# Perceiver stack on one core: the second layer's first two blocks in one stage each, projections moved from the middle chain beside its maxima, a row bias, and unread products left out

## The chip, the cores and the metric

One core of one Trainium2 chip. The metric is the device time of one execution in microseconds (us), median of the runs. Engines: PE is TensorE, DVE is VectorE, ACT is ScalarE, POOL is GpSimd, SP is SyncE, which issues the DMAs.

## The reference

Two layers over a state `x` of 128 rows and 256 columns. Each layer is cross attention of `x` on a context of 12544 rows, then a small self block, then a feed forward block with quantised weights. Cut to what matters:

```
x = x + L0_xattn(ln(x), ctx, mask)       # 16 heads of 16, keys 12544, mask, softmax
x = x + L0_attn(ln(x))                   # causal linear attention, its FFN (gelu)
x = x + L0_ffn(ln(x))                    # bit-linear: gate, up, down
x = x + L1_xattn(ln(x), ctx, ctx)        # 16 heads, keys 12544, no mask
x = x + L1_attn(ln(x))                   # RWKV mix: Wk, Wv, Wr, a scan over the rows, Wo
x = x + L1_ffn(ln(x))                    # bit-linear w1, conv over 3 rows, silu, w2
```

In cross attention `q = (ln(x) Wq + bq) * 0.25`, keys `ctx Wk + bk`, values `ctx Wv`, and the softmax over all 12544 keys is made block by block with a running maximum for each head and query.

## The kernel before, in words

The keys are cut into 98 tiles of 128, these into blocks of 8 tiles, NG = 13 blocks a layer (the last of 2 tiles). Block m of layer l is m = NG * l + n, so blocks 0 to 12 are layer 0, block NG = 13 is the first of layer 1. All engines run programs written out by hand with semaphores. For each tile PE makes

- `scores`: first the running maximum is subtracted by a product with `minus16` (L1574), then keys times queries (L1578) into the four banks of `ps_scores`; ACT takes the exponential (L821; in layer 0 with a mask added before it);
- `weigh` (L1599) of the tile before: values times probabilities, added up in `ps_out`;
- `projections`: one unit, either 512 columns of keys of block m + 2 (`keys_in`, L1516) or two tiles of values of block m + 1 (`values_in`, L1501), in four strips of 32 into `ps_proj`;
- `maxima`: products of rounded keys and queries (L1523), whose largest over 512 keys VectorE finds (L1099 in layer 0, L1102 in layer 1). A block has 32 of them, for the block after: the table `count_at(m, t)` says how many stand behind the scores, behind the weighing and at the end of tile t, for this block (`own`), the next (`now`) and the one after (`ahead`).

When a block's 32 maxima are done VectorE joins them to the running maximum (`chain`, L1143), ACT rounds it (`max_out`, L773), PE spreads it over rows (`turn_max`, L1618), ACT copies it (`rows_out`, L797), POOL takes the change and ACT its exponential (`decay_out`, L789), and VectorE scales `ps_out` by it (`decay_sums`, L1166). This is a stage. In layer 0 and for most of layer 1 a stage is a block. Blocks NG and NG + 1 are **split** in two stages of four tiles (`is_split`, SPLIT = 4, `CHAINS`): before layer 1's first tile only the 16 maxima over block NG's first four tiles are made, two at a time (`pair_maximum`, L1134), and its other 16 go behind its tiles 0 to 2 (`own`).

Between the layers lies the **middle chain**: a chain of small steps of PE, VectorE and ACT (self block and feed forward). PE fills its waits in program order with projection units of blocks NG, NG + 1 and NG + 2, here at full width (`keys_whole` L1487, `values_whole` L1477): `BETWEEN` lists 13 of them, `between_in(...)` places them, ACT copies them out (`between_out`). Three more, in strips, stand beside the pair maxima (`BESIDE`, after pairs 2, 5 and 7).

Behind the last tile comes the **closing chain**: the last weighing, the turn of the sums (L1610), `wo` (L1463), the RWKV products (L1855, L1860, L1862), the products by `w1` (L1876), the convolution's PE half (L1885), the turns of the hidden rows (L1890, L1896) and `w2` (L1901). `idle_products(n)` (L1677) issues n products of 256 columns whose result nobody reads; one of them shows as two MATMUL instructions in the trace, as every f32 product does.

At the start SP loads, in this order: x, Wq, Wk, bk, half of the first context block, bq (one row of 256 copied to all 128 partitions, L481), the other half, the mask, Wv and so on. VectorE adds bq to the query product (L1216) and scales the two halves into `qz` (L1223). PE's order there is: query product, the first key unit, the turn of `qz` (L1703), the second key unit, then the maxima.

`lends(m, t)` picks maxima of layer 1 that ACT copies out of PSUM first (L764), so that VectorE reads the copy (L1109).

## Time and profile before

| | us |
|---|---|
| median of 3 runs (963.69 to 967.66) | 963.81 |
| the profiled execution | 969.17 |
| its span, first to last instruction | 966.3 |
| PE busy | 924.5 (96%) |
| VectorE busy | 755.6 (78%) |
| ACT busy | 697.8 (72%) |
| POOL busy | 398.6 (41%) |

The span divides into: the start up to the first tile (38 us), layer 0's tiles (to 461 us), the middle chain (462 to 510), the pair maxima (510 to 520), layer 1's tiles (521 to 925) and the closing chain (925 to 966). The chain of waits that ended last is 83% PE, 7% VectorE, 3% ACT. An engine's busy share says what it did, not what it held up; the chain says the latter.

### The profile page before, as it was taken

The numbers are of one execution on the slowest core, as the hardware profiler recorded it, in microseconds if no ns is written. First come the engines' busy times: TensorE is split into PE (matmuls) and PEld (weight loads), VectorE is DVE, ScalarE is ACT, GpSimd is POOL, SyncE is SP. The second block draws the span as 40 slices with busy tenths as digits, with TensorE's granted clock in tenths as the row PEclk, the third lists the DMA queues.
The fourth block names the chain that finished last, engine by engine and source line by source line (L and its number), as shares of the span: only waits on it lengthen the run. The fifth ranks groups of instructions, "written<-read, shape, count | busy, mean of one in ns | idle before, by whom it ended". The sixth has DMA issues, their size and how long they took to land.

```text
span 966.3 us, 37466 instructions
## 1 busy us (share of the span) xinstructions
PE 924.5 (96%) x16290; PEld 572.3 (59%) x16291; DVE 755.6 (78%) x1610; ACT 697.8 (72%) x1005; POOL 398.6 (41%) x365
## 2 busy tenths in 40 slices
PE   7999999999999999999888899999999999999987
PEld 3455665665656566655563556666666666666666
DVE  5888888888888888967446988777777778777666
ACT  3678998998998899897563456666666666666752
POOL 4368888788888877886100010021202000110000
PEclk9999999999999999999997999999999999999999
DMA  8411201201211110123005001011101101000000
GB/s 337 165 42 67 88 26 68 90 24 68 89 60 55 67 58 8 68 91 134 6 26 193 2 2 46 3 45 46 45 4 46 46 3 46 14 3 3 3 1 6
DMA packets 14995, 53.08 MB, mean 55 GB/s; under 512 B 4336, under 2 KB 5744, under 8 KB 10992
## 3 DMA queue, kind: packets, MB, share of 16 engines
q1 hardware_dynamic: 14832, 50.70, 15.1%
q8 instruction: 128, 2.10, 0.9%
q14 instruction: 35, 0.29, 0.1%
HBM read 50.56 MB, written 0.13 MB: 52 GB/s over the span
## 4 chain that ended last, share of the span: by engine, by line
PE 83%; DVE 7%; issue 5%; ACT 3%; DMA 1%; POOL 0%; SPq 0%; DVEq 0%; POOLq 0%; ACTq 0%
PE ps_out L1599 18%; PE ps_scores L1578 16%; PE ps_proj L1501 15%; PE ps_proj L1516 14%; PE ps_max L1523 7%; PE ps_scores L1574 4%; DVE tile_max L1102 2%; ACT probs L821 1%; PE ps_proj L1523 1%; DVE probs L1194 1%; PE ps_scores L1516 1%; DMA bq<-in_L_xattn_bq 1%; DVE unread L1099 1%; PE ps_out L1477 1%; PE ps_max L1477 1%
## 5 line engine op out<-in xcount | busy, mean ns | idle before, releaser
L637 POOL TENSOR_TENSOR probs<-probs,masks 128x512 f32<-128x512 f32 x180 | 227.3, 1284 | 76.3 <-ACT probs L807 76.3
L815 ACT ACTIVATE probs<-probs 128x1024 f32<-128x1024 f32 x196 | 206.7, 1055 | 44.7 <-DVE probs L1183 34.1
L1578 PE MATMUL ps_scores<-q_pad,k_full 32*128 32x256 f32 x3072 | 237.3, 378 | 0.0
L1099 DVE CUSTOM_DVE_ANT_0 unread<-ps_max,masks 128x512 bf16<-128x512 f32 (+1 forms) x294 | 190.5, 675 | 49.1 <-PE ps_max L1523 48.2
L821 ACT ACTIVATE probs<-ps_scores 128x1024 f32<-128x1024 f32 x192 | 186.3, 1021 | 44.8 <-PE ps_scores L1578 44.4
L1599 PE MATMUL ps_out<-probs,values 128*32 128x128 f32 x6272 | 217.1, 277 | 1.6 <-DVE ps_out L1166 0.5
L1578 PEld LDWEIGHTS ps_scores<-q_pad,k_full 32*128 32x128 f32 x3072 | 187.0, 187 | 12.5
L1599 PEld LDWEIGHTS ps_out<-probs,values 128*32 128x32 f32 x6272 | 159.3, 110 | 57.3 <-issue 50.4
L1501 PE MATMUL ps_proj<-wv,ctx_t 128*32 128x256 f32 x2752 | 165.3, 381 | 0.2
L1523 PE MATMUL ps_max<-k_high,q_high 32*128 32x512 bf16 (+1 forms) x579 | 153.2, 382 | 8.5 <-DVE tile_max L1099 3.2
L1516 PE MATMUL ps_proj<-ctx_t,wk 128*32 128x512 f32 (+1 forms) x1360 | 159.8, 587 | 1.0 <-DVE tile_max L1099 0.8
L628 POOL CAST k_high<-k_full 128x1024 bf16<-128x1024 f32 (+1 forms) x51 | 50.2, 988 | 215.6 <-DVE k_full L1118 116.5
L1102 DVE TENSOR_REDUCE tile_max<-ps_max 128x1 f32<-128x512 f32 (+1 forms) x202 | 134.0, 671 | 6.0 <-PE ps_max L1523 5.2
L643 POOL TENSOR_TENSOR max_step<-max_rows 128x512 f32<-128x512 bf16 x26 | 30.1, 1159 | 214.2 <-ACT max_rows L797 214.2
L1574 PE MATMUL ps_scores<-max_rows,minus 32*128 32x512 bf16 x768 | 109.9, 382 | 6.5 <-ACT probs L821 4.4
L1523 PEld LDWEIGHTS ps_max<-k_high,q_high 32*128 32x128 bf16 x579 | 37.7, 91 | 132.0 <-DVE tile_max L1099 52.9
L1501 PEld LDWEIGHTS ps_proj<-wv,ctx_t 128*32 128x32 f32 x2752 | 81.8, 110 | 50.1 <-DVE tile_max L1099 0.8
L1183 DVE TENSOR_TENSOR probs<-ps_scores,masks 128x1024 f32<-128x1024 f32 x90 | 109.7, 1219 | 0.0
L764 ACT CAST unread<-ps_max 128x512 bf16<-128x512 f32 (+1 forms) x79 | 45.6, 577 | 83.9 <-PE ps_max L1523 83.9
L807 ACT COPY probs<-ps_scores 128x512 f32<-128x512 f32 x180 | 95.4, 584 | 1.4 <-PE ps_scores L1578 1.3
L1102 DVE TENSOR_REDUCE tile_max<-ps_proj 128x1 f32<-128x512 f32 (+1 forms) x103 | 69.4, 674 | 15.0 <-PE ps_max L1523 8.0
L1523 PE MATMUL ps_proj<-k_high,q_high 32*128 32x512 bf16 (+1 forms) x193 | 72.3, 375 | 3.2 <-DVE tile_max L1102 3.2
(308 smaller groups left out, 940.8 us busy)
## 6 DMA issues: line engine op xcount, KB each, us to landing
ctx_t<-in_ctx_t SPq DMA_DIRECT2D x23, 1024.0 KB, 5.9
masks<-in_mask_n SPq DMA_DIRECT2D x12, 512.0 KB, 3.7
masks<-in_mask_t SPq DMA_DIRECT2D x12, 512.0 KB, 3.9
room_w<-in_L_attn_f_w SPq DMA_DIRECT2D x2, 1024.0 KB, 7.0
room_w<-in_L_ffn_w SPq DMA_DIRECT2D x2, 1024.0 KB, 8.1
ctx_t<-in_ctx_t SPq DMA_DIRECT2D x2, 512.0 KB, 5.7
room_w<-in_L_ffn_w_gate SPq DMA_DIRECT2D x1, 1024.0 KB, 11.1
room_w<-in_L_ffn_w_up SPq DMA_DIRECT2D x1, 1024.0 KB, 13.6
```

The source lines that it names most:

```text
L637: nc.gpsimd.tensor_tensor(p, p, three(mask_t[m % 2], GT)[:, t, :].unsqueeze(1).to_broadcast([P, 4, P]), ALU.add).then_inc(sig("bias_added" ...
L815: nc.scalar.activation(prob(T, half), prob(T, half), ACT.Exp).then_inc(sig(f"exp_done{half}"), 1)
L821: nc.scalar.activation(prob(T, half), scores_in(m, t, half).rearrange("p a n -> p (a n)"), ACT.Exp).then_inc(sig(f"exp_done{half}"), 1)
L1099: ins = v.tensor_tensor_reduce(unread[:, j % 2, 0:width(m)], max_bank(m, j)[:, 0:width(m)], mask_n[m % 2][:, half_cols(m, half)], 1.0, -3e ...
L1102: ins = v.tensor_reduce(tile_max[:, h, 1 + half:2 + half], max_bank(m, j)[:, 0:width(m)], AX_X, ALU.max)
L1183: v.tensor_tensor(prob(T, 0).rearrange("p (h q) -> p h q", h=8), ps_scores[:, 0:2, :].rearrange("p a (h q) -> p (a h) q", q=P), three(mask ...
L1501: last = mm(bank[32 * g:32 * (g + 1), D * (t - at.start):D * (t - at.start + 1)], ctx_t[m % 3][:, t, c, keys], wv[l][:, c, :], start=(c == ...
L1516: last = mm(bank[32 * g:32 * (g + 1), 0:width(m)], wk[l][:, c, dims], ctx_t[m % 3][:, 4 * half:min(4 * half + 4, size(m)), c, :], start=(c ...
L1523: mm(bank[:, 0:width(m)], q_high[rows, c, zz, :], k_high[m % 2][rows, c, half_cols(m, half)], start=True, stop=True).then_inc(sig("max_rea ...
L1574: mm(banks[g], minus16[rows, :], max_rows[stage(m, t) % 2][rows, :], start=True, stop=True)
L1578: last = mm(banks[g][:, D * c:D * (c + 1)], k_full[m % 3][rows, c, P * t:P * (t + 1)], q_pad[rows, c, :], start=False, stop=True, skip_gro ...
L1599: last = mm(ps_out[VW * g:VW * (g + 1), P * c:P * (c + 1)], values[m % 2][:, t, h, :], prob(T, half)[:, P * o:P * (o + 1)], start=(t == 0 ...
```

## The change

Six parts:

1. **One stage for each of the blocks NG and NG + 1.** `is_split` is always false, `CHAINS` is empty. All 16 pairs of maxima of block NG are made before layer 1's first tile; its 32 maxima for block NG + 1 go 4, 6, 6, 6, 4, 4, 2 behind tiles 0 to 6, and block NG + 1 has the table of the later blocks. Two chains, turns, row copies and scalings go.
2. **Projections.** `BETWEEN` has 9 units in place of 13, `BESIDE` 7 in place of 3, one after each odd pair from 1 to 13.
3. **Idle products.** All 44 calls behind layer 1's last weighing and in the closing chain are left out. Before `turn_max` of the opening there are 7 in place of 1, and 2 new ones behind it.
4. **bq of layer 0** is loaded as one row of one partition, second behind Wq, and added by PE with a product of one row of ones. VectorE's addition goes.
5. `lends` asks that the next tile has a projection (three copies by ACT for the last two blocks' maxima go, and block NG + 1 has six where it had four), and layer 0's late addition of `bv` and scaling of layer 1's bq (L1263, L1265) move from block NG - 2, tile 4, to block NG - 3, tile 3.
6. PE's wait for `sums_taken` behind the sums of layer 0 goes; in ACT's program some copies of units stand behind the step of the chain that they stood ahead of; pairs of waits ahead of one instruction change places.

```diff
-        bq = [sb(f"bq{l}", [P, D]) for l in range(2)]
+        bq_row = sb("bq_row", [1, D])
+        bq = sb("bq", [P, D])
...
         def is_split(m):
-            return m in (NG, NG + 1)
+            return False
...
-        CHAINS = {(NG, SPLIT - 2): NG + 1, (NG, 5): NG + 2, (NG, 7): NG + 3}
+        CHAINS = {}
...
             if m == NG:
-                own = ((2, 2, 2), (2, 2, 2), (2, 2, 0))[t] if t < SPLIT - 1 else own
-                now = ((0, 0, 0), (0, 0, 0), (0, 0, 4), (2, 2, 2), (2, 2, 2), (2, 2, 2), (2, 2, 2), (2, 2, 0))[t]
-            elif m == NG + 1:
-                now = (2, 2, 2) if t in (2, 4) else (2, 0, 2) if t < chain_at(m) else (2, 0, 0) if t == chain_at(m) else now
+                now = (2, 2, 2) if t in (1, 2, 3) else (2, 0, 2) if t < chain_at(m) else (2, 0, 0) if t == chain_at(m) else now
...
-            if m <= NG or k >= BLOCKS or lone(k, s):
+            if m <= NG or k >= BLOCKS or lone(k, s) or not (keys_at(k, s) or values_at(k, s)):
...
-        BIAS_AT = NG - 2
+        BIAS_AT = (NG - 3, 3)
...
-        BETWEEN = [("k", NG + 1, 0), ("k", NG + 1, 1), ("v", NG, 0), ("v", NG, 1), ("v", NG, 2), ("k", NG + 1, 2), ("k", NG + 1, 3),
-                   ("k", NG + 2, 0), ("v", NG, 3), ("v", NG + 1, 0), ("v", NG + 1, 1), ("v", NG + 1, 2), ("k", NG + 2, 1)]
+        BETWEEN = [("k", NG + 1, 0), ("k", NG + 1, 1), ("v", NG, 0), ("k", NG + 1, 2), ("k", NG + 1, 3), ("v", NG, 1),
+                   ("v", NG, 2), ("v", NG, 3), ("k", NG + 2, 0)]
-        BESIDE = [("k", NG + 2, 2), ("k", NG + 2, 3), ("v", NG + 1, 3)]
-        BESIDE_AT = (2, 5, 7)
+        BESIDE = [("k", NG + 2, 1), ("v", NG + 1, 0), ("k", NG + 2, 2), ("v", NG + 1, 1), ("k", NG + 2, 3), ("v", NG + 1, 2), ("v", NG + 1, 3)]
+        BESIDE_AT = (1, 3, 5, 7, 9, 11, 13)
...
+                if l == 0:
+                    project(ps_proj[:, 0:D], wq[0], whole=False)
+                    pe.wait_ge(sig("q_bias0"), 16)
+                    pe.wait_ge(sig("ones_set"), 1)
+                    mm(ps_proj[:, 0:D], ones[0:1, :], bq_row[0:1, :], start=False, stop=True).then_inc(sig("q_ready"), 1)
...
                 if l == 1:
-                    idle_products(1, ps_proj)
+                    idle_products(7, ps_proj)
                 turn_max(NG * l, ps_proj)
...
+                    idle_products(2)
...
-                    between_in(0, 1, 2)
-                pe.wait_ge(sig("sums_taken"), l + 1)
+                    between_in(0, 1)
...
-                    between_in(4)
...
-                    between_in(5, 6)
+                    between_in(3)
...
-                    between_in(9, 10, 11)
+                    between_in(6, 7)
...
-            idle_products(1)
+            pe.wait_ge(sig("sums_taken"), 2)
...
-            idle_products(3)
...
-            idle_products(4)
...
-            idle_products(18)
...
-            idle_products(7)
...
-            idle_products(2)
...
-                idle_products((1, 6)[half])
```

How the instructions stand, at three places. On SP at the start, before:

```order
L521 DMA x<-in_x 128x256
L510 DMA wq<-in_L_xattn_Wq 128x512
L515 DMA wk<-in_L_xattn_Wk 128x512
L516 DMA bk<-in_L_xattn_bk 128x2
L495 DMA ctx_t<-in_ctx_t 128x1024
L481 DMA bq<-in_L_xattn_bq 128x256
L495 DMA ctx_t<-in_ctx_t 128x1024
L500 DMA masks<-in_mask_n 128x1024
```

and now:

```order
L516 DMA x<-in_x 128x256
L505 DMA wq<-in_L_xattn_Wq 128x512
L518 DMA bq_row<-in_L_xattn_bq 1x256
L510 DMA wk<-in_L_xattn_Wk 128x512
L511 DMA bk<-in_L_xattn_bk 128x2
L490 DMA ctx_t<-in_ctx_t 128x1024 x2
L495 DMA masks<-in_mask_n 128x1024
```

The broadcast of 128 rows ahead of the second half of the context is gone; Wk, bk and the first half each stand one issue later, the second half where it stood.

On PE in layer 1's opening, from the pair maxima (k_high, q_high) to the first tile's scores (rows of wk and wv are units of `BESIDE`, those of wq and ident are idle products), before:

```order
L1523 MATMUL ps_scores<-k_high,q_high 128x512 x4
L1523 MATMUL ps_max<-k_high,q_high 128x512 x2
L1516 MATMUL ps_out<-ctx_t,wk 32x512 x8
L1523 MATMUL ps_scores<-k_high,q_high 128x512 x4
L1523 MATMUL ps_max<-k_high,q_high 128x512 x2
L1516 MATMUL ps_proj<-ctx_t,wk 32x512 x8
L1523 MATMUL ps_scores<-k_high,q_high 128x512 x4
L1501 MATMUL ps_out<-wv,ctx_t 32x256 x16
L1677 MATMUL ps_proj<-wq,ident 128x256
L1618 MATMUL ps_proj<-ident,max_of_head 32x128 x16
L1574 MATMUL ps_scores<-max_rows,minus 128x512 x4
```

and the last part of it now:

```order
L1515 MATMUL ps_scores<-k_high,q_high 128x512 x4
L1493 MATMUL ps_out<-wv,ctx_t 32x256 x16
L1515 MATMUL ps_max<-k_high,q_high 128x512 x2
L1515 MATMUL ps_scores<-k_high,q_high 128x512 x2
L1669 MATMUL ps_proj<-wq,ident 128x256 x7
L1610 MATMUL ps_proj<-ident,max_of_head 32x128 x16
L1669 MATMUL ps_out<-wq,ident 128x256 x2
L1566 MATMUL ps_scores<-max_rows,minus 128x512 x4
```

Ahead of this part stand 24 maxima and six units, so that 32 maxima and seven units now precede the first scores, where 16 and three did.

On PE in the closing chain, from `wo` to the products by w1, before:

```order
L1463 MATMUL ps_proj<-wo,xn_t 128x256 x2
L1677 MATMUL ps_out<-wq,ident 128x256 x3
L1452 MATMUL ps_max<-ident,xn 128x128 x2
L1677 MATMUL ps_out<-wq,ident 128x256 x4
L1855 MATMUL ps_scores<-room_t,room_w 128x128 x12
L1677 MATMUL ps_out<-wq,ident 128x256 x18
L1860 MATMUL ps_proj<-room_w,room_t 128x256
L1862 MATMUL ps_proj<-room_w,room_t 128x256
L1677 MATMUL ps_out<-wq,ident 128x256 x7
L1866 MATMUL ps_max<-ident,room_t 128x128 x2
```

and now:

```order
L1455 MATMUL ps_proj<-wo,xn_t 128x256 x2
L1444 MATMUL ps_max<-ident,xn 128x128 x2
L1849 MATMUL ps_scores<-room_t,room_w 128x128 x12
L1853 MATMUL ps_proj<-room_w,room_t 128x256
L1855 MATMUL ps_proj<-room_w,room_t 128x256
L1858 MATMUL ps_max<-ident16,room_t 128x128 x2
```

Only the products that are read are left.

## Rows read from the trace of the kernel before

**Rows 1.** Start, DMA issues at 3.09 and 3.56 us (size, us to landing)
```profile
bq<-in_L_xattn_bq SPq DMA_DIRECT2D x1, 128.0 KB, 6.7
...
ctx_t<-in_ctx_t SPq DMA_DIRECT2D x1, 512.0 KB, 7.6
```

**Rows 2.** Start, timeline (start us, us, engine, line, operation, [idle before])
```profile
6.94 1.92 PE L1516 MATMUL ps_scores<-ctx_t,wk 128*32 128x512 f32 x16
...
9.90 0.42 DVE L1216 TENSOR_TENSOR room_t<-ps_proj,bq 128x256 f32<-128x256 f32 x1 [4.66 <-DMA bq<-in_L_xattn_bq]
...
10.78 0.66 PE L1703 MATMUL ps_max<-ident,room_t 128*128 128x128 f32 x4 [1.91 <-DVE room_t L1223]
```

**Rows 3.** Middle chain, timeline of PE and VectorE (DVE)
```profile
465.93 0.41 DVE L1302 TENSOR_SCALAR xn<-x,stat 128x256 f32<-128x256 f32 x1
...
466.15 1.89 PE L1477 MATMUL ps_max<-wv,ctx_t 128*128 128x256 f32 x8
...
474.59 0.42 DVE L1320 COPY room_t<-ps_proj 128x256 f32<-128x256 f32 x1 [0.86 <-PE ps_proj L1789]
...
479.57 1.88 PE L1487 MATMUL ps_max<-ctx_t,wk 128*128 128x512 f32 x4
...
479.87 0.41 DVE L1031 TENSOR_SCALAR xn<-room_t,stat 128x256 f32<-128x256 f32 x1
...
500.62 0.43 DVE L1067 TENSOR_SCALAR masks<-probs 128x512 bf16<-128x512 f32 x1
```

**Rows 4.** Second layer's opening, timeline: pair maxima, a projection, an idle product
```profile
510.53 2.36 DVE L1134 TENSOR_REDUCE tile_max<-ps_scores 128x2 f32<-128x1024 f32 x2 [1.92 <-PE ps_scores L1523]
...
516.66 1.93 PE L1501 MATMUL ps_out<-wv,ctx_t 128*32 128x256 f32 x32
...
518.52 0.70 PE L1677 MATMUL ps_proj<-wq,ident 128*128 128x256 f32 x2
...
521.34 0.62 PE L1574 MATMUL ps_scores<-max_rows,minus 32*128 32x512 bf16 x4 [0.74 <-issue]
...
525.48 1.22 PE L1677 MATMUL ps_out<-wq,ident 128*128 128x256 f32 x2
```

**Rows 5.** Three stretches: us, busy us of PE, PEld, DVE, ACT, POOL, granted clock, DMA
```profile
517.95:521.36 3.41, 1.69 (x34) 0.71 (x27) 1.91 (x3) 1.49 (x4) 0.00 (x0) 1.00 0.53 144
521.36:531.60 10.24, 9.39 (x85) 5.37 (x85) 5.06 (x8) 5.26 (x6) 0.00 (x0) 0.50 0.14 57
925.00:966.30 41.30, 33.61 (x199) 26.56 (x195) 27.29 (x83) 14.72 (x27) 3.08 (x5) 0.99 0.01 4
```

**Rows 6.** PE timeline: first rows of tiles, and the turns of the maxima (L1618)
```profile
547.65 0.50 PE L1574 MATMUL ps_scores<-max_rows,minus 32*128 32x512 bf16 x4
...
551.35 0.50 PE L1574 MATMUL ps_scores<-max_rows,minus 32*128 32x512 bf16 x4
...
557.57 0.41 PE L1618 MATMUL ps_max<-ident,max_of_head 128*32 128x128 bf16 x16
...
593.76 0.41 PE L1618 MATMUL ps_max<-ident,max_of_head 128*32 128x128 bf16 x16
...
627.28 0.41 PE L1618 MATMUL ps_max<-ident,max_of_head 128*32 128x128 bf16 x16
...
880.05 0.60 PE L1574 MATMUL ps_scores<-max_rows,minus 32*128 32x512 bf16 x4
...
883.35 0.40 PE L1574 MATMUL ps_scores<-max_rows,minus 32*128 32x512 bf16 x4 [0.50 <-ACT probs L821]
```

**Rows 7.** PE timeline of the closing chain
```profile
934.79 2.94 PE L1855 MATMUL ps_scores<-room_t,room_w 128*128 128x128 f32 x24 [0.55 <-DVE room_t L1372]
...
937.57 7.94 PE L1677 MATMUL ps_out<-wq,ident 128*128 128x256 f32 x36
...
951.33 1.07 PE L1876 MATMUL ps_scores<-xn_t,ctx_t 128*128 128x128 bf16 x16
...
956.58 0.66 PE L1890 MATMUL ps_scores<-ident,masks 128*128 128x128 f32 x4 [0.23 <-ACT masks L993]
```

More of the change, by code:

```diff
@@ L196, in is_split @@
         def is_split(m):
-            return m in (NG, NG + 1)
+            return False
         def stage(m, t=0):
-            return m + max(0, min(m - NG, 2)) + int(is_split(m) and t >= SPLIT)
+            return m
         def in_stage(m, t):
@@ L206, in block_of @@
         def block_of(s):
-            m = s - max(0, min((s - NG + 1) // 2, 2))
-            return m, is_split(m) and stage(m) == s
+            return s, False
         def tiles_to(s):
@@ L296, in count_at @@
                 now = (2, 0, 2 if t < chain_at(m) else 0)
-            if m == NG:
-                ahead = (0, 0, 2) if t == size(m) - 1 else ahead
-            elif n + 2 < NG:
+            if n + 2 < NG:
                 ahead = (0, 0, 2) if t == chain_at(m) else (2, 0, 2) if t > chain_at(m) else ahead
@@ L342, in perceiver @@
         for l in range(2):
-            done = {NG * l: (2 * H, H)[l]}
-            read = {bank: ("max_free", maxima0(NG * l) + (2 * H, H)[l]) for bank in range(2)}
+            done = {NG * l: 2 * H}
+            read = {bank: ("max_free", maxima0(NG * l) + 2 * H) for bank in range(2)}
             order, turned_here, moved = [0, 1, 2], {}, 0
@@ L511, in load_q_weights @@
                 if l == 1:
-                    row(bq[l][:, :], f"L{l}_xattn_bq", D, "q_bias1")
+                    row(bq[:, :], f"L{l}_xattn_bq", D, "q_bias1")
             def load_k_weights(l):
@@ L522, in _ @@
             load_q_weights(0)
+            sp.dma_start(bq_row[:, :], a["L0_xattn_bq"].rearrange("(o n) -> o n", o=1)).then_inc(sig("q_bias0"), 16)
             load_k_weights(0)
             load_first_ctx(0)
-            row(bq[0][:, :], "L0_xattn_bq", D, "q_bias0")
             load_first_ctx(1)
@@ L1233, in _ @@
                 else:
-                    for i in range(H // 2):
+                    for i in range(H):
                         pair_maximum(NG, i)
@@ L1459, in turn_apart, with project @@
                 return last
-            def project(dst, w, src=xn_t):
+            def project(dst, w, src=xn_t, whole=True):
                 for c in range(DC):
-                    last = mm(dst, src[:, c, :], w[:, c, :], start=(c == 0), stop=(c == DC - 1))
+                    last = mm(dst, src[:, c, :], w[:, c, :], start=(c == 0), stop=whole and c == DC - 1)
                 return last
@@ L1698, in _ @@
                 if l == 1:
[L1699 to L1700 removed]
+                    between_read(7)
+                    between_read(8)
                 for zz in range(2):
@@ L1720, in _ @@
                 else:
-                    for i in range(H // 2):
+                    for i in range(H):
                         pair_maximum(NG, i)
@@ L1724, in _ @@
                             beside_in(BESIDE_AT.index(i))
-                    beside_read(1)
+                    for u in (len(BESIDE) - 2, len(BESIDE) - 1):
+                        if u % 2 == 1:
+                            beside_read(u)
                 read_by[0] = ("max_copied", NG * l + 1)
                 if l == 1:
-                    idle_products(1, ps_proj)
+                    idle_products(7, ps_proj)
                 turn_max(NG * l, ps_proj)
                 if l == 1:
-                    beside_read(2)
+                    for u in (len(BESIDE) - 2, len(BESIDE) - 1):
+                        if u % 2 == 0:
+                            beside_read(u)
+                    idle_products(2)
                 if l == 0:
```

66 lines of the change are left out of this document (29 added, 37 removed).

## The prediction

> **What bounds the kernel now.** I read the page first: PE is busy in 96% of the span and makes 83% of the chain of waits, so in the long run of tiles only PE's own work counts, and there the change does nothing. What it touches are four places where PE is not the whole chain: the start, the middle chain, layer 1's opening and the closing chain. For each I read the timeline of PE beside those of VectorE and ACT, and for the clock the table of stretches.
>
> At the start VectorE has the query product at about 7.4 us and waits until 9.9 for bq, whose copy to 128 partitions lands 6.7 us after its issue; the second half of the context is queued behind it and lands at 3.56 + 7.6 = 11.2 us [rows 1, 2]. In the middle chain the small steps are often ready before PE has ended the full-width unit ahead of them: ln1's result is there at 466.34, a unit begun at 466.15 ends 1.7 us later; ln2's is there at 480.28, a unit begun at 479.57 is ahead of it [rows 3]. In the opening VectorE's reductions follow each other without a hole (about 1.14 us a pair, two in 2.36), and PE has time for units beside them [rows 4]. Then the clock: in 517.95 to 521.36 PE was busy for half the time, at full clock, and the next 10.2 us were granted 0.50, the lower of the two levels (1.2 GHz of 2.4), though PE was busy for 9.4 of them. The closing chain is at 0.99 [rows 5].
>
> **The change part by part.** All times against the profiled execution (969.17, span 966.3), which lies 5.4 us above the median of the runs; I take the same difference for both.
>
> *Start: -1.4.* The query product ends where the first unit begins now, at 6.94, and the row bias adds one product, two instructions of 0.215 [rows 7] (36 in 7.94, with the end of the last): q is ready at 7.4. VectorE's 0.42 addition and its wait to 9.9 go, and PE's turn of qz then stands behind its own first unit, 7.4 + 1.9 = 9.3, where it began at 10.78 [rows 2]: 1.45 earlier. The second unit needs the context's second half by 10.0 and not by 11.4. I take it that it lands in time, since the 128 rows of bq that held the queue are gone; Wk and the first half come one issue later (0.47) and are not late. Bounds: 0.2 if that half lands where it did, 1.45. In the Trainium skill, "DMA: Bandwidth & Descriptors", section Specifications, pieces of 512 bytes or more move at line rate; by that bq's 1 KB rows took some 0.3 us of the queue, the half would land at 10.9 and this part would give 0.5, not 1.4. The rows speak for more: bq, a quarter of the half's size, landed 6.7 us after its issue, and the half only 1.4 us behind it.
>
> *Middle chain: -4.7.* Four units of 1.72 leave it (6.9 us of PE). In each gap I let PE begin the next step at the later of its units' end and its input [rows 3]. First gap, three units to two: the turn waited for the third unit to 467.9, its input is there at 466.34, but ACT first copies the second unit (0.7 from 466.3): 1.3. Behind the attention product (a unit fewer): the copy that PE must wait for ends at 475.01, and PE, in a unit since the product ended (about 474.5), came to it at 476.2: 1.15. Before ln2's turn: 481.3 against 480.28: 1.1. ACT's new order ahead of the quantised rows: 0.2. Before the turn of the hidden rows (three units to two): the second half's input is there at 501.05 and PE was some 0.9 behind it. Sum 4.7; bounds 3.9 (ACT's copies in the way each time) and 6.9.
>
> *Opening: -0.8.* The pairs: 16 x 1.14 = 18.3 us in place of 9.15, all VectorE. Beside them PE makes seven units of 1.86, 13.0 us, and has 5.3 for 32 small products, as before 3.6 for 16 [rows 4]: VectorE stays the bound, +9.15. The seven idle products are 3.0 us and begin about 2.4 before VectorE ends, so they end with the rounding of the maxima; the two behind the turn take 0.86 where ACT's row copy took 0.7: +0.2. Then the first block's tiles. Before, from 521.34 to the turn of the next block's maxima at 557.57, they took 36.2 [rows 4, 6] at 48 maxima, 10 us of it at the lower level. Now: 32 maxima. A tile with six is 3.7 (547.65 to 551.35, VectorE's bound), one with four and no projection 3.3 (880.05 to 883.35, where PE waited for ACT) [rows 6]. 3.3 + 3 x 3.7 + 3 x 3.3 for tiles 0 to 6 and 1.7 of tile 7 up to the turn = 26.0: -10.2. I take the full clock: PE is dense through the pairs. Bounds of this part: +4 (the lower clock for the same 10 us) and -3.
>
> *Block NG + 1: -2.7.* From turn to turn it took 593.76 - 557.57 = 36.2, the next block 627.28 - 593.76 = 33.5 [rows 6]. The table is now the same, and the scaling within the block is gone. Bounds 0 and 2.7.
>
> *Small parts: +0.3.* VectorE's 1.3 us for `bv` and bq moves from a tile where it had an idle stretch behind it to one where it has 0.6: 0 to 0.7. The copies that `lends` drops stood while ACT waited for PE: nothing. Two turns, copies and scalings fewer are in the two blocks above. Waits that change places: nothing.
>
> *Closing chain: +5.8.* The 44 idle products are 88 x 0.215 = 18.9 of the 33.6 us that PE is busy there [rows 5, 7], and one call, between the two turns of the hidden rows (0.43), is on the path. Without them PE is busy for 14.7 of 41, 36%, less than the half that went before the fall in the opening. So I expect the lower level from about 929 on. What streams then doubles, of it on the path: the turn ahead of wo and wo itself 0.11 + 0.86, the next turn 0.21, the first 8 of the 24 RWKV products 8 x 0.107 = 0.86 (the other 16 stay hidden behind VectorE's scans), two products of Wo 0.86, the small turns 0.15, 8 of the 16 by w1 0.43: 3.5. The 24 products of the convolution ended just before ACT released the turns at 956.58 (0.23 of wait): doubled (2.6 more) they end later than ACT by all but its wait and their fill: +2.1. The turns of both halves +0.86 less the idle 0.43, the last turn 0.21, w2 0.43. Sum 6.6. I take 5.8, since 5 us of convolution without a gap may lift the clock, as 10 dense us did at 531.6. Bounds: -0.4 (no fall) and +6.6.
>
> **Sum:** -1.4 - 4.7 - 0.8 - 2.7 + 0.3 + 5.8 = -3.5. The profiled execution would be 965.7 and the median 960.3.
>
> **The rivals.**
> 1. *The clock stays up longer in the closing chain.* The Trainium skill, "TensorE: Matmul & The Clock Gate", section Why this matters for your kernels, warns of long idle gaps between bursts of matmuls alone; by that rule the first loss would come in the hole of 8 us before the products of Wo. As a mechanism here: wo, the turns and the RWKV products (2.1 of the 6.6) stay at full, the rest pays 4.5 less 0.8, time 958.2. Against it stands the fall at 521.36, with no hole over 1 us ahead of it [rows 4, 5]: the trace does not agree with that rule. With no fall at all: 960.3 - 6.2 = 954.1. Chances 0.12 and 0.06.
> 2. *The middle chain loses the clock.* Between the attention products and ln2 a unit of 1.7 is gone twice, and PE would be busy for about two thirds, in the sparsest part for half. One fall doubles wo of the self block (4 x 0.215), a unit (1.7) and part of the f1 products: some 3 us, time 963.3. Against it: the gaps of the same chain before did not lose the clock. Chance 0.15.
> 3. *The opening gives less:* the first tile of block NG + 1 or the 4-maxima tiles wait for ACT longer, and the saving of 3.5 there halves: 962. Chance 0.12.
> 4. *Slower.* The clock falls before the pairs, in the gaps around qz, and strips of 32 and 32-row products do not lift it again. A unit is then 3.6, seven are 25 us, 7 more than VectorE's 18.3, and the first tiles pay 3 more: 960.3 + 10 = 970.3. It decides if the granted clock is under 1 for most of the pairs. For it: the lower level lasted 10 us at PE 92% busy [rows 5]. Against: all of layer 0 runs on such strips at full clock. Chance 0.07.
> 5. That the change does not do what it says: the order of instructions shows each part; none.
>
> **How the numbers follow.** My case has 0.48. The likeliest time is 960.3. A difference of 0.5% (4.8 us) is about what a measurement of this kernel can tell from none, so faster means under 959.0, slower over 968.6. Faster: rival 1 (0.16 of its 0.18) and the early part of my case (0.14): 0.30. Slower: rival 4 and a sum of misses, 0.08. Same: 0.62. Range: my bounds on the start, the opening and the clock give 956 to 964; with rivals 2 and 3 and part of 1, 955.5 to 966.0.
>
> **What would show it.** Right: the first VectorE operation on q near 7.5 us; ln1's turn about 3 us and the first query product of layer 1 about 6 us earlier than now; VectorE without a hole over 16 pairs; granted clock 1.00 through the first block, whose tiles take 26 us to the turn; next block 3 us shorter; 0.50 from some 4 us behind the last weighing, and a closing chain near 47 us in place of 41. Wrong: a closing chain at full clock, a clock of 0.5 in the middle chain or the pairs, or a first block over 29 us.

## The result, and the profile after

The changed kernel takes 967.34 us (median of 20 runs, 963.67 to 971.24), the kernel before 964.41 (20 runs beside them; 18 lie between 962.6 and 968.5, two took 1918 and 1996 us): ratio 1.0026, 95% interval 1.0015 to 1.0036. A second series gave 967.04 against 964.60, 1.0018 (1.0003 to 1.0032). By the medians it is slower by 2.4 to 2.9 us, well below the 0.5% that I called the limit of a measurement, and I had forecast 3.5 faster.

The profiled execution took 966.25 us with a span of 963.6. That is **2.7 us less** than the span of the profiled execution of before (966.3), and close to the 965.7 that I had worked out for it. It is also 1.9 less than the median span of the 20 runs of the changed kernel (965.5). So the two profiles say faster, the medians slower, and the experiments had to say which is right.

The page of the changed kernel first, its row of the granted clock:

```profile
PEclk9999999999999999999999999999999999999965
```

It is full up to the last two slices; before, the dent was in the middle, in layer 1's opening. The start, timeline of PE and then VectorE, against [rows 2] and the query product of before:

```profile
5.88 1.13 PE L1463 MATMUL ps_proj<-wq,xn_t 128*128 128x256 f32 x4
```

and now:

```profile
5.72 2.07 PE L1455 MATMUL ps_proj<-wq,xn_t 128*128 128x256 f32 x4
7.73 0.69 PE L1688 MATMUL ps_proj<-bq_row,ones 1*128 1x256 f32 x2
8.35 1.92 PE L1508 MATMUL ps_scores<-ctx_t,wk 128*32 128x512 f32 x16
10.21 0.66 PE L1701 MATMUL ps_max<-ident,room_t 128*128 128x128 f32 x4
...
8.53 0.49 DVE L1215 TENSOR_SCALAR room_t<-ps_proj 128x128 f32<-128x128 f32 x2 [3.35 <-PE ps_proj L1688]
```

VectorE begins on q at 8.53, where it began at 9.90; the wait for bq is gone. But the query product's four instructions take 2.07 us where they took 1.13, and the bias product 0.69. Layer 1's side, the middle chain to the first tile (ln1's turn, ln2's turn, the turn of the hidden rows, the turn of q, the turn of the maxima, the first tile), against [rows 3, 4]:

```profile
465.35 0.33 PE L1450 MATMUL ps_scores<-ident,xn 128*128 128x128 f32 x1
...
476.95 0.33 PE L1450 MATMUL ps_scores<-ident,xn 128*128 128x128 f32 x1 [0.61 <-DVE xn L1024]
...
495.73 0.40 PE L1827 MATMUL ps_max<-ident,masks 128*128 128x128 bf16 x4 [0.42 <-DVE masks L1060]
...
503.25 0.66 PE L1701 MATMUL ps_max<-ident,room_t 128*128 128x128 f32 x4 [0.21 <-DVE room_t L1217]
...
523.89 0.41 PE L1610 MATMUL ps_proj<-ident,max_of_head 128*32 128x128 bf16 x16 [0.27 <-ACT max_of_head L768]
...
525.29 0.39 PE L1566 MATMUL ps_scores<-max_rows,minus 32*128 32x512 bf16 x4
```

ln1's turn came at 467.88 in the trace of before and q's turn at 508.63: they are 2.5 and 5.4 earlier. From there to the first tile it takes 22.0 us, as forecast 9.3 more than the 12.7 before (521.34 - 508.63). The turns of the next two blocks' maxima and the first score product of the last tile, against [rows 6]:

```profile
551.82 0.41 PE L1610 MATMUL ps_max<-ident,max_of_head 128*32 128x128 bf16 x16
...
585.06 0.41 PE L1610 MATMUL ps_max<-ident,max_of_head 128*32 128x128 bf16 x16
...
912.41 0.39 PE L1566 MATMUL ps_scores<-max_rows,minus 32*128 32x512 bf16 x2 [0.88 <-ACT probs L816]
```

The first block takes 26.5 us to the turn (forecast 26.0), the second 33.24 (forecast 33.5). The last tile began at 921.11 before, so everything ahead of the closing chain gives 8.7 us; my terms for it sum to 9.3. Then stretches, against [rows 5] (us, busy us of PE, PEld, DVE, ACT, POOL, granted clock, DMA):

```profile
503.00:524.00 21.00, 19.83 (x235) 9.02 (x238) 18.62 (x19) 5.70 (x10) 1.04 (x1) 1.00 0.51 201
524.00:552.00 28.00, 24.74 (x456) 16.03 (x453) 22.44 (x37) 16.92 (x20) 0.00 (x0) 1.00 0.02 6
918.00:933.00 15.00, 8.74 (x32) 6.91 (x32) 7.95 (x32) 5.11 (x9) 1.35 (x2) 0.54 0.00 0
933.00:936.00 3.00, 0.00 (x0) 0.00 (x0) 2.91 (x7) 2.24 (x3) 0.64 (x1) 1.00 0.00 0
936.00:953.00 17.00, 9.10 (x44) 7.52 (x45) 11.41 (x33) 5.26 (x12) 1.09 (x2) 0.50 0.00 0
953.00:956.00 3.00, 1.78 (x13) 1.30 (x12) 1.75 (x4) 0.53 (x2) 0.00 (x0) 0.97 0.00 0
```

The pairs and the first block have the full clock. The closing chain has the lower level from about 919, and gets the higher back twice, for some 3 us each: at 932.7, as the dense RWKV products end (927.64 + 5.34), where PE has nothing to do and cannot use it, and at 953. The steps on the path there, against [rows 7]:

```profile
920.45 2.05 PE L1455 MATMUL ps_proj<-wo,xn_t 128*128 128x256 f32 x4 [0.54 <-ACT xn_t L729]
924.67 0.69 PE L1444 MATMUL ps_max<-ident,xn 128*128 128x128 f32 x2 [2.17 <-DVE xn L1024]
927.64 5.34 PE L1849 MATMUL ps_scores<-room_t,room_w 128*128 128x128 f32 x24 [2.28 <-DVE room_t L1364]
939.53 1.22 PE L1853 MATMUL ps_proj<-room_w,room_t 128*128 128x256 f32 x2 [6.55 <-POOL room_t L696]
...
945.02 0.40 PE L1858 MATMUL ps_max<-ident,room_t 128*128 128x128 bf16 x2 [3.41 <-DVE room_t L1060]
...
948.55 2.93 PE L1876 MATMUL ps_scores<-masks,tern 128*128 128x128 f32 x12 [0.78 <-DVE masks L1413]
...
953.52 1.28 PE L1881 MATMUL ps_scores<-ident,masks 128*128 128x128 f32 x8
957.48 0.61 PE L1886 MATMUL ps_max<-ident,room_t 128*128 128x128 bf16 x4 [2.67 <-DVE room_t L1060]
```

The 24 RWKV products take 5.34 where they took 2.94, and PE waits 6.5 us for POOL ahead of Wo and 3.4 for VectorE ahead of the next turn: the holes that the idle products had filled. From the last tile's first score product to the end it is 963.6 - 912.41 = 51.2 us, where it was 45.2.

### The profile page after: what moved, and what is told of

It reads as the page before. It is cut to its first block, busy times and chain, and to the rows that moved or that the text cites. A ratio compares the mean times of both kernels' runs of the same rounds, so it can differ in the third digit from the quotient of the medians.

```text
span 963.6 us, 37392 instructions
## 1 busy us (share of the span) xinstructions
PE 911.5 (95%) x16272; PEld 559.3 (58%) x16273; DVE 753.9 (78%) x1597; ACT 694.3 (72%) x994; POOL 396.9 (41%) x363
## 4 chain that ended last, share of the span: by engine, by line
PE 84%; DVE 6%; issue 6%; ACT 4%; POOL 0%; DMA 0%; DVEq 0%; POOLq 0%; ACTq 0%
PE ps_out L1591 18%; PE ps_scores L1570 16%; PE ps_proj L1493 15%; PE ps_proj L1508 14%; PE ps_max L1515 7%; PE ps_scores L1566 4%; ACT probs L816 2%; PE ps_scores L1508 1%; DVE probs L1187 1%; DVE unread L1092 1%; PE ps_out L1508 1%; PE ps_proj L1455 1%; ACT probs L810 0%; PE ps_max L1610 0%; PE ps_scores L1799 0%
## 5 line engine op out<-in xcount | busy, mean ns | idle before, releaser
L1570 PE MATMUL ps_scores<-q_pad,k_full 32*128 32x256 f32 x3072 | 233.8, 374 | 0.0
L1092 DVE CUSTOM_DVE_ANT_0 unread<-ps_max,masks 128x512 bf16<-128x512 f32 (+1 forms) x294 | 190.5, 675 | 47.3 <-PE ps_max L1515 46.4
L1570 PEld LDWEIGHTS ps_scores<-q_pad,k_full 32*128 32x128 f32 x3072 | 184.3, 185 | 12.4
L1493 PE MATMUL ps_proj<-wv,ctx_t 128*32 128x256 f32 x2848 | 171.2, 381 | 0.2
L1515 PE MATMUL ps_max<-k_high,q_high 32*128 32x512 bf16 (+1 forms) x573 | 149.5, 379 | 6.0 <-DVE tile_max L1092 3.6
L623 POOL CAST k_high<-k_full 128x1024 bf16<-128x1024 f32 (+1 forms) x51 | 50.6, 996 | 199.5 <-DVE k_full L1111 114.7
L1095 DVE TENSOR_REDUCE tile_max<-ps_max 128x1 f32<-128x512 f32 (+1 forms) x191 | 127.0, 670 | 5.4 <-PE ps_max L1515 4.2
L638 POOL TENSOR_TENSOR max_step<-max_rows 128x512 f32<-128x512 bf16 x24 | 27.9, 1162 | 224.6 <-ACT max_rows L792 224.6
L1493 PEld LDWEIGHTS ps_proj<-wv,ctx_t 128*32 128x32 f32 x2848 | 84.6, 110 | 52.4 <-DVE tile_max L1092 0.8
L1095 DVE TENSOR_REDUCE tile_max<-ps_proj 128x1 f32<-128x512 f32 (+1 forms) x99 | 66.7, 674 | 13.4 <-PE ps_max L1515 6.6
L1515 PE MATMUL ps_proj<-k_high,q_high 32*128 32x512 bf16 (+1 forms) x189 | 69.8, 369 | 0.2
```

The source lines that it names most:

```text
L1092: ins = v.tensor_tensor_reduce(unread[:, j % 2, 0:width(m)], max_bank(m, j)[:, 0:width(m)], mask_n[m % 2][:, half_cols(m, half)], 1.0, -3e ...
L1095: ins = v.tensor_reduce(tile_max[:, h, 1 + half:2 + half], max_bank(m, j)[:, 0:width(m)], AX_X, ALU.max)
L1493: last = mm(bank[32 * g:32 * (g + 1), D * (t - at.start):D * (t - at.start + 1)], ctx_t[m % 3][:, t, c, keys], wv[l][:, c, :], start=(c == ...
L1515: mm(bank[:, 0:width(m)], q_high[rows, c, zz, :], k_high[m % 2][rows, c, half_cols(m, half)], start=True, stop=True).then_inc(sig("max_rea ...
L1570: last = mm(banks[g][:, D * c:D * (c + 1)], k_full[m % 3][rows, c, P * t:P * (t + 1)], q_pad[rows, c, :], start=False, stop=True, skip_gro ...
```

## The experiments

Each kernel ran with the kernel before on the same chip: e1 to e4 on one, f1 to f4 on a second, g1 to g4 on a third. Between these groups only the ratios to before compare. The first four:

### e1: the changed kernel with the closing chain's idle products

```diff
+            idle_products(18)
             pe.wait_ge(sig("wkv_first"), 1)
```

and so at all ten places, 44 calls (the diff shows one).

> The changed kernel with all 44 idle products of the closing chain put back, as the kernel before has them. Theory A (the profiled execution of before was not a typical one: its stretch at the lower clock in layer 1's opening, worth some 5 us, is missing in most executions, so the opening's gain was never there; the closing chain lost what I forecast): the closing chain, from the first score product of the last tile to the end, is 45 us again instead of 51, granted clock 0.99 or more, and the time is 6 us below the change's 967.3, about 961.5, some 3 below before. Rival B (the closing chain is not what costs, the middle chain or opening of the changed kernel falls to the lower clock in most executions): the time stays above 964 and the granted clock of the runs at 0.99 or less. Rival C (the idle products only hold up the path): no gain, 967.

962.44 us (12 runs), ratio to before 0.9974 (0.9959 to 0.9990). Against the changed kernel's 967.34 that is 4.9 us: theory A. From the last tile to the end it is 960.7 - 915.54 = 45.2 us again. Rival C falls, and so does rival B, which asked for more than 964 us or a clock of 0.99 or less. The profile had something else in it, at the start:

```profile
5.85 2.07 PE L1455 MATMUL ps_proj<-wq,xn_t 128*128 128x256 f32 x4
7.86 1.22 PE L1688 MATMUL ps_proj<-bq_row,ones 1*128 1x256 f32 x2
9.00 3.64 PE L1508 MATMUL ps_scores<-ctx_t,wk 128*32 128x512 f32 x16
12.58 1.12 PE L1701 MATMUL ps_max<-ident,room_t 128*128 128x128 f32 x4
...
40.76 0.40 PE L1566 MATMUL ps_scores<-max_rows,minus 32*128 32x512 bf16 x4 [0.41 <-issue]
```

These are the same instructions at twice their duration: the unit of 16 takes 3.64 us instead of 1.92, q's turn begins at 12.58 instead of 10.21, and the first tile comes at 40.76 instead of 37.68. The table of stretches does not show it, because the trace's record of the clock has its first entry only where the full speed comes (here at 14.19 us), and what lies ahead of that entry counts as full (first row; the second is the closing chain, at 0.99 again):

```profile
5.80:14.20 8.40, 8.37 (x31) 3.18 (x34) 0.52 (x3) 1.16 (x2) 3.58 (x5) 1.00 1.00 370
920.00:960.70 40.70, 33.12 (x194) 26.30 (x193) 27.31 (x83) 14.25 (x27) 3.08 (x5) 0.99 0.01 4
```

The 12 spans fall in groups: three of 957.8 to 958.7 us at a granted clock of 0.998 or more, five of 959.9 to 960.7 at the same clock (the profiled one with its late first tile is of these), and four of 963.2 to 963.6 at 0.995 to 0.996. The clock alone does not sort them: f2 below, with the old start, has 959.5 to 960.4 at 0.998 to 0.999, and 961.1 and 961.2 at 0.996.

### e2: the kernel before without its closing idle products

```diff
-            idle_products(18)
             pe.wait_ge(sig("wkv_first"), 1)
```

> The kernel before without the 44 idle products behind the second layer's last weighing and in its closing chain. Theory A: it loses 5.8 to 6.0 us and ends near 970.3; the products that stream at the lower clock double, the chain from the last tile's first score is 51 us. Rival C: 964 or less. Rival B says nothing of its own here.

968.77 us (6 runs), ratio 1.0041 (1.0026 to 1.0055). From the other side the price is 3.6 us by the medians and 4.5 against e3; by the trace 5.6 (967.8 - 916.98 = 50.8 from the last tile to the end). Both are under the 5.8 to 6.0 that were expected.

### e3: the kernel before, once more

> The kernel before itself, unchanged, to see how its executions spread and at what granted clock. Theory A: ratio 1.000; most executions at a granted clock of 0.997 or more and a span near 961.5, few at 0.992 with a span near 966; in the new profile the first score products behind the 16-head opening (from about 521 us) run at full clock and the first block's tiles take about 31 us to the turn of the next maxima instead of 36. Rival D (the lower clock in the opening is in most executions, and the spread has another cause): clock 0.992 in most, whatever the span.

964.26 us (12 runs), ratio 0.9995 (0.9982 to 1.0008). Its profile (timeline; then stretches) shows what I had not known of the kernel that I started from:

```profile
5.86 2.05 PE L1463 MATMUL ps_proj<-wq,xn_t 128*128 128x256 f32 x4
...
10.64 0.66 PE L1703 MATMUL ps_max<-ident,room_t 128*128 128x128 f32 x4 [0.48 <-DVE room_t L1223]
...
521.24 0.40 PE L1574 MATMUL ps_scores<-max_rows,minus 32*128 32x512 bf16 x4 [0.74 <-issue]
...
553.50 0.41 PE L1618 MATMUL ps_max<-ident,max_of_head 128*32 128x128 bf16 x16
...
917.11 0.39 PE L1574 MATMUL ps_scores<-max_rows,minus 32*128 32x512 bf16 x2 [0.88 <-ACT probs L821]
```

```profile
518.00:521.20 3.20, 1.52 (x30) 0.54 (x19) 1.76 (x3) 1.43 (x4) 0.00 (x0) 1.00 0.52 125
521.20:531.60 10.40, 8.94 (x143) 5.78 (x143) 8.75 (x15) 6.96 (x8) 0.06 (x1) 1.00 0.16 65
533.00:541.00 8.00, 6.90 (x106) 4.80 (x109) 6.22 (x11) 3.56 (x7) 1.15 (x1) 0.79 0.01 2
```

The stretch of 10.2 us at clock 0.50 behind the opening [rows 5] is not there; a fall of 3.4 us near 535 is. The first block takes 553.50 - 521.24 = 32.3 us, not 36.2. In the runs beside these experiments and of e3, 100 in all, before's spans follow the granted clock of the whole run: 961.4 us at 0.999, 963.4 at 0.996, 965 at 0.994, 966.3 at 0.992. Eight of the 100 are at 0.992 or less. The profile I had argued from, 966.3 at 0.992, is like those few. Theory A holds, rival D falls. The short fall of 3.4 us is no accident of this execution: by the clock's record it is there in all four profiles with the old opening (538.4 in before, 534.2 in e2, 534.4 here, 532.4 in e4), and in none of the nine that have the new opening with its idle products.

### e4: the kernel before with the new start alone

```diff
-            row(bq[0][:, :], "L0_xattn_bq", D, "q_bias0")
+            sp.dma_start(bq_row[:, :], ...)
...
+                    mm(ps_proj[:, 0:D], ones[0:1, :], bq_row[0:1, :], start=False, stop=True).then_inc(sig("q_ready"), 1)
```

> The kernel before with the changed start alone (bq as a row of one partition, loaded ahead of Wk, and added by one product behind the query product). My forecast for this part was -1.4; the profile of the changed kernel showed -0.6 at the turn of q and -0.6 at the first tile, because its query products took 2.07 us instead of 1.13. If those slow products belong to the new order of loads: -0.6. If they were that one execution's: -1.4, and the query products are at 1.1 us here.

964.15 us (12 runs), ratio 0.9997 (0.9982 to 1.0012): no gain at all. In the profile the query products took 1.58, q's turn began at 9.77 and the first tile at 37.23, 1.06 earlier than in before. Of the eight runs at clock 0.997 or 0.998, four have spans of 960.9 to 961.7 and four of 964.1 to 964.7. The kernel before shows no such pair of groups at one clock in its 100 runs.

### f1 to f4: which part of the start splits the runs

f1 and f2 put the old start back into the changed kernel, without and with the closing idle products. f3 and f4 are e1 with one part of the start altered: f3 leaves the one-row product out (layer 0's query bias is missing, so its output is wrong), f4 keeps it and lets VectorE wait as long as before, which was to give PE its gap back:

```diff
+                if l == 0:
+                    dve.wait_ge(sig("first_ctx1"), 16)
```

> The changed kernel with the start of the kernel before (bq copied to 128 partitions behind the context's first half, VectorE adds it). Seen so far: with the new start the executions of one granted clock fall into two groups 3 us apart, with the old start they do not, and one profile with the new start has its products from 5.8 to about 14 us at twice their duration, its first tile at 40.8 instead of 37.7. Theory S (the new start brings this slow stretch in more than half of the executions): one group at granted clock 0.982, span 962.2 to 962.7, median time 965 (2 below the change), ratio to before 1.001 or less; first tile at 38.2. Rival T (the two groups have nothing to do with the start): two groups 3 us apart remain, median 967.5 to 968.

> The changed kernel with the closing chain's idle products and the start of the kernel before: what is left of the change is the middle chain and the unstaged opening with its idle products. From the landmarks of the profiles (middle chain -4.3, opening from q's turn to the first tile +9.3, first block -5.7, second block -3.0) it is 3.7 us under before at the same granted clock: span 958.0 at 0.998, ratio 0.996. Theory S: one group per clock, median time 961 or less, no worse than the 962.4 of the kernel with the new start. Rival T: two groups 3 us apart, as with the new start.

> The changed kernel with the closing chain's idle products, its new order of loads, but without the one-row product that adds bq (layer 0's query bias is left out). Which part of the new start brings the slow stretch? If it is the one-row product (PE works with one row of 128 for 0.7 to 1.2 us in the middle of the stretch): one group per clock, first tile at 37.0 to 37.5, spans about 957.3 at 0.998. If it is that PE's turn of q and the second unit follow without the gap of two us that the kernel before has there, or the order of the loads: two groups 3 us apart stay.

> The changed kernel with the closing chain's idle products; VectorE's scaling of q also waits for the second half of the first context, so that PE has a gap behind its first unit as before, with the one-row product kept. If the missing gap brings the slow stretch: one group per clock, first tile near 38, median 961 to 961.5. If it is the one-row product or the loads: two groups stay, the late one still 2 to 3 us behind, median 962.5 to 963.

| kernel | median us | ratio to before (95%) | spans, us |
|---|---|---|---|
| f1 | 967.50 | 1.0035 (1.0022 to 1.0048) | 964.3 to 967.5 |
| f2 | 961.79 | 0.9969 (0.9956 to 0.9981) | 958.2 to 961.2 |
| f3 | 960.42 | 0.9959 (0.9944 to 0.9974) | 958.1 to 959.3 |
| f4 | 962.97 | 0.9981 (0.9964 to 0.9997) | 958.2 to 961.5, and five of 963.1 to 963.4 |

With the old start or without the one-row product there is no late group (28 runs). With the product and VectorE's wait it stays, and f4's profile, timeline, is such an execution, its first tile at 40.53:

```profile
8.95 3.64 PE L1510 MATMUL ps_scores<-ctx_t,wk 128*32 128x512 f32 x16
```

That f4's span is 963.4 has a second cause: the clock's record has two falls of 3.4 us in layer 0 (at 54.8 and 413.2), and layer 0 took 426.5 us instead of 423.5. The early runs of f4 at the same clock of 0.996 have 960.2 and 960.9.

So the late group goes with the product, and not with the order of the loads, which f3 shares. On the gap f4 says less than it was made for: in this execution the first unit ended at 12.5, after VectorE's wait (over at 9.34), so PE had no gap. It shows only that VectorE's wait does not prevent the late start.

f1 missed its number: 967.5, where I expected 965. With the old start the changed kernel has no late group and is no faster for it (ratio 1.0035, with the new start 1.0026 and 1.0018; the intervals overlap). I had started from the changed kernel's fastest spans (961.7) instead of its profile (963.6, first tile 37.68); f1's profile is 964.3 with its first tile at 37.95, and f2 plus the 6.0 of the closing chain is 967.8.

### g1 to g4: the repair, and what the idle products of the opening do

g1 (with the closing idle products) and g4 (without) add the bias by a product over all 128 rows, 127 of them zero:

```diff
-                    mm(ps_proj[:, 0:D], ones[0:1, :], bq_row[0:1, :], start=False, stop=True).then_inc(sig("q_ready"), 1)
+                    mm(ps_proj[:, 0:D], ones[:, :], bq_row[:, :], start=False, stop=True).then_inc(sig("q_ready"), 1)
```

g2 is the changed kernel again; g3 is e1 without the 9 idle products of the opening.

> The changed kernel with the closing chain's idle products, and bq's row added by a product over all 128 rows (127 of them zero) instead of one row; order of loads and everything else as in the new start. Theory S2 (the product with one row of 128 is what lets the slow stretch at the start go on to about 14 us): one group of executions per granted clock, first tile at 37.0 to 37.7, lowest span near 957.5, median time 960.5 or less, ratio to before near 0.996. Rival (what matters is that there is any product more in that place): late executions near 963.2 stay and the median is 962.5.

> The changed kernel once more, for the spread of its executions and a second profile. From the 20 runs seen: granted clock 0.977 to 0.982, spans in an early group (961.7 to 963.8) and a late one (965.1 and more), the late one in about two thirds; median 967.3. If the profile falls into the late group, S2 expects the products from 5.8 to about 14 us at twice their duration and the first tile near 40.8; a late profile with its first tile at 37.7 would speak against it.

> The changed kernel with the closing chain's idle products, but without the 9 idle products of its own opening (7 ahead of the turn of the maxima, 2 behind it). If they hold the clock there: the granted clock falls to 0.5 near 524 to 530 in most executions, as in the profiled execution of before, spans 3 to 5 us longer, median 965 to 967. If the pairs with their seven units keep PE dense enough: nothing is lost and the opening is 0.2 us shorter, median 962.4 as with them.

> The changed kernel with nothing altered but the bias product, over all 128 rows as above; the closing chain is without idle products. By S2 alone the late group goes and the spans are 961.7 to 963.8, median 964.5. But the changed kernel with the old start, which has no late group either, had 967.5 with its fastest span at 964.3. If the price of the bare closing chain depends on when the lower clock sets in against the chain, the fast start shifts that too: then anything from 961.5 to 966 for the fastest span, and the closing chain's length, 51.2 us in both profiles so far, differs from profile to profile by some 2 us with the granted clock.

**g1: 959.81 us** (5 runs, spans 957.8 to 958.3), ratio 0.9942 (0.9927 to 0.9958): the fastest kernel here, 4.8 us under before and 7.2 under the changed kernel beside it (g2). Five runs are few: if half of all executions were late, 1 in 32 such sets would show none. Its start, timeline of PE:

```profile
5.76 1.13 PE L1457 MATMUL ps_proj<-wq,xn_t 128*128 128x256 f32 x4
6.72 0.59 PE L1690 MATMUL ps_proj<-bq_row,ones 128*128 128x256 f32 x2
7.25 1.92 PE L1510 MATMUL ps_scores<-ctx_t,wk 128*32 128x512 f32 x16
9.10 0.66 PE L1703 MATMUL ps_max<-ident,room_t 128*128 128x128 f32 x4
...
36.62 0.40 PE L1568 MATMUL ps_scores<-max_rows,minus 32*128 32x512 bf16 x4 [0.41 <-issue]
```

This is the start as I had forecast it: VectorE has q at 7.43 (forecast 7.4), and the first tile comes 1.67 us before that of the kernel before. Its middle chain, though, has a fall of the kind of my rival 2 (stretch of 6 us; granted clock 0.72). From the sums of layer 0 to q's turn it took 43.0 us where the changed kernel took 42.1 (g4's profile has the same fall at 474.2 and took 43.2):

```profile
472.00:478.00 6.00, 5.06 (x12) 2.51 (x11) 2.53 (x9) 2.39 (x5) 0.00 (x0) 0.72 0.00 0
```

**g2:** 967.04 us (12 runs). At clock 0.982 one span of 962.5 and three of 964.8 to 965.3. The profile fell on the early one: first tile at 37.09, and 50.6 us from the last tile to the end. It could not test the late group.

**g3:** 964.82 us (12 runs), ratio 0.9990 (0.9973 to 1.0007), which overlaps e1's interval; but all 12 runs have a clock of 0.996 or less, where 8 of e1's 12 have 0.998 or more. Without the opening's idle products it is 2.4 us over e1 by the medians, 1.5 by the ratios, and 3.0 by the two profiles, which have the same late first tile (963.7 against 960.7). In its profile, stretches behind the pairs:

```profile
524.00:527.00 3.00, 0.00 (x0) 0.00 (x0) 2.81 (x4) 0.12 (x1) 0.86 (x1) 0.90 0.91 292
527.00:536.50 9.50, 8.53 (x84) 4.92 (x88) 3.37 (x6) 5.31 (x8) 0.00 (x0) 0.50 0.05 21
```

PE had nothing to do for 3 us while VectorE ended its pairs, and then 9.5 us at the lower clock, busy for 8.5 of them; the first block took 29.4 us to the turn instead of 26.5. This is the fall of [rows 5] in another kernel.

**g4:** 966.83 us (12 runs), ratio 1.0022 (1.0009 to 1.0035), fastest span 962.7. From the last tile to the end 50.7. Its start was again slow up to 9.9 us, into the first unit (2.54 us against 1.92):

```profile
5.78 2.08 PE L1457 MATMUL ps_proj<-wq,xn_t 128*128 128x256 f32 x4
...
8.64 2.54 PE L1510 MATMUL ps_scores<-ctx_t,wk 128*32 128x512 f32 x16
11.11 0.65 PE L1703 MATMUL ps_max<-ident,room_t 128*128 128x128 f32 x4
```

The first tile came at 38.62. So the product over all rows does not shorten the slow start in every execution; that this one was long is not explained by anything I tried.

## Why the prediction was wrong

**The step that failed first is the basis:** "All times against the profiled execution (969.17, span 966.3), which lies 5.4 us above the median of the runs; I take the same difference for both." The changed kernel's profiled execution (966.25) lies 1.1 us below its median, not 5.4 above it. That is nearly the whole miss: the same profile, less the 5.4 that I took, is 960.9, and the median is 967.34. Of the 5.4, 4.0 us were the lower clock behind the opening (36.2 against 32.3 us in the first block), and the change takes away just the tiles in which it lay (another 1.1 lie outside the span: 2.9 between span and time, where 1.8 is the median). I put the gain of that fall into the sum and then kept its cost in the difference. Against the twin (e3, span 962.3), which is an ordinary execution, the same terms give:

| part | forecast, against the profile of before | after, against e3 | measured |
|---|---|---|---|
| start, to the first tile | -1.4 | 37.68 - 38.15 | -0.5 |
| layer 0 | 0 | 423.5 - 424.0 | -0.5 |
| middle chain, sums to q's turn | -4.7 | 42.1 - 46.4 | -4.3 |
| q's turn to the first tile | +9.3 | 22.0 - 12.7 | +9.3 |
| first block | -10.2 | 26.5 - 32.3 | -5.7 |
| second block | -2.7 | 33.24 - 36.20 | -3.0 |
| the rest of layer 1 | 0 | 327.4 - 327.4 | 0 |
| closing chain | +5.8 | 51.2 - 45.2 | +6.0 |
| sum | -3.5 | 963.6 - 962.3 | +1.3 |

(The forecast column sums to -3.9; +0.3 of small parts and rounding make the -3.5.) The small parts do not show as a term of their own. Without the fall, the unstaged opening and the second block together are worth +0.6, not -3.5: the change buys nothing there. Even the -5.7 of the first block holds the short fall near 535, which the old opening has in all four profiles; an estimate of its worth is half of its 3.4 us, 1.7.

**The second is the start, "-1.4".** VectorE's wait for bq was read rightly, and the trace of before had the query product at full speed (1.13 us). I did not see that this too is a matter of the execution. In all the profiles PE's first products run at half speed (in the changed kernel's the first turn of two takes 0.69 us at 4.57, the same turn 0.44 at 500.57). The full speed, where the clock's record begins, comes at 5.6 to 5.9 us in before, f3 and g1, at 6.5 and 7.7 in the changed kernel's two profiles, at 6.8 in e4, at 8.4 to 8.7 in e2, e3, f1 and f2, at 9.9 in g4 and at 13.8 to 14.4 in e1, f4 and g3. With the old start this is hidden up to about 10.5 us, by the very wait that the change removes: q's turn begins at 10.78 in before, 10.64 in e3 and 10.51 in e2.

The one-row product begins at 7.1 to 7.9. In the three profiles in which the full speed was there by then (g2, e4 and, just, the changed kernel's first) nothing more was lost. In the three in which it was not (e1, f4, g3) it came only at about 14, and the first tile was 3.1 later (40.8 against 37.7). Without that product no profile had to wait beyond 8.7, or 9.9 with the product over all rows. How often the long form comes is read from groups of spans and is uncertain: 5 of 12 in f4, 4 of 8 in e4, 4 to 9 of 12 in e1.

What the start is worth as a whole the direct pairs say: e4 against before 0.9997 (0.9982 to 1.0012), f1 in place of the changed kernel 1.0035 for 1.0026, f2 in place of e1 0.9969 for 0.9974. It is about nothing; -1.4 us (a ratio of 0.9985) lies just inside e4's interval. **What stays open** is the rest: the table gives +1.3 for two single executions, and the medians say 2.4 to 2.9. Half of 3.1 for late starts would fill the difference, but f1, which has no late group, has as high a median (967.50). No run separates the late start from the other things that differ between executions of a kernel with a bare closing chain.

**What held.** The middle chain: -4.3 of -4.7. The opening: +9.3, VectorE's 16 pairs without a hole. The second block. And the closing chain, term by term, each read as the distance between two starts: wo with the turns on both its sides +1.55 up to the RWKV products (forecast 1.2), these and the wait up to Wo +0.9 (0.9), Wo up to the next turn +0.7 (0.9), the small turns and w1 +0.7 (0.6), the convolution +1.8 (2.1), the turns behind it -0.2 (+0.4; at 953.5 the clock was back for them, 8 in 1.28), the last products +0.6 (0.6). The clock fell near 919, some 3 us behind the last weighing, where I had said 4.

**The rivals.** Rival 1 (the clock holds in the closing chain) did not come in any profile of a kernel without the idle products: the granted clock of those runs is 0.977 to 0.982. Rival 2 did not come in the changed kernel's two profiles, but in g1 and g4 at a third of its price (0.9 and 1.1). Rival 4 (970.3 us, a clock below full in the pairs) was the wrong mechanism: the pairs had 1.00. What did work on that side, an untypical basis and a wait whose removal uncovers PE's slow start, I had not listed. My range ended 1.3 us below the median.

## What to carry to other kernels

Before taking a gain from a stretch at the lower clock, ask whether that stretch is in most executions: compare the profiled execution's own time and granted clock with the spread of the runs, and if it lies at the edge, take the fall out of the basis first. Products that nothing reads may be the cheapest thing in a chain of small steps: here 44 calls of 0.43 us, all but one off the path, save 3.6 to 7 us by the medians of four pairs of kernels, 5.4 to 6 by their traces. And a wait that looks idle at the start of a kernel may be covering an engine that is not yet at speed; after removing it, look at the durations of the same instructions and not at the clock's row.

## What the runs showed of the hardware

- The granted clock's row read 1.00 over 8.4 us in which every product took twice its time (e1: 3.64 us for 16 against 1.92). At the start of this program the row says nothing, because the record's first entry is the rise to full speed (5.6 to 14.4 us in the 14 profiles); durations tell. The Trainium skill, "TensorE: Matmul & The Clock Gate", Part 1, says that the throttled state is the default and that activity releases it, and that the number of slow products at a kernel's start varies from run to run. The traces agree, which show its end between 5.6 and 14.4 us.
- That page puts the price of the slow start under 1% of a kernel's span. It is: 3.1 us are 0.3%. It is also more than the whole effect of this change.
- One product whose operands have one row of 128 (0.7 to 1.2 us) went with the long form of the slow start: in the profiles of e1, f4 and g3, and by their late groups in the changed kernel and e4. The 28 runs of f1, f2 and f3, without it, and the 5 of g1, with 127 rows of zeros beside it, have no late group; g4's profile has the slow start up to 9.9 us all the same. By what mechanism one row matters was not tried.
- The granted clock changed behind PE's activity, not with it. It rose at 932.7, as the dense RWKV products ended, and was up for 3.4 us in which PE had almost nothing to do. In g3 it fell at 526.4, in a hole of 3.6 us without a product, and stayed low for 10.2 us, of which PE was busy for 8.7. The Trainium skill's same page, section Why this matters for your kernels, warns of gaps of more than about 3 us between bursts. g3 agrees with that; the closing chain's fall at 919 came behind a gap of 0.8 us and within one of 1.5, which that warning does not cover.
